# V's product in double groups with a twelve-slot ring of probabilities, and layer norms cut into stages

## The reference

```python
x = x + L0_xattn(layernorm(x), ctx)   # 8 heads of 8 channels, band |q-k| <= 64, gated with ctx
x = x + L0_ffn(layernorm(x))          # ternary 256x256 weight, tanh-scaled by the row norm
x = x + L1_xattn(layernorm(x), ctx)   # rotary, full 256x256 scores, keys and values of mixed origin
x = x + L1_ffn(layernorm(x))          # 256 -> 1024 -> 256, 4-bit weights with LoRA, relu

# attention, per sequence and head
scores = q @ k.T / sqrt(8);  p = softmax(scores);  o = p @ v
# layernorm
(x - mean) / sqrt(var + 1e-5)
```

## Time and profile before

| | us |
|---|---|
| three runs, median (lowest to highest) | 1336.01 (1335.77 to 1337.31) |
| the profiled execution | 1332.8 |
| its span | 1331.0 |
| TensorE's mean granted clock in it | 0.984 of full |

### The profile page before, as it was taken

One profiled execution on the slowest core, in us unless ns is written; L12 is line 12 of the kernel. 1 busy time (PEld: TensorE's weight loads), 2 busy tenths in 40 slices (PEclk: granted clock), 3 DMA queues, 4 the chain that ended last, 5 costly groups with the idle time before them and its releaser, 6 DMA issues.

```text
span 1331.0 us, 35488 instructions
## 1 busy us (share of the span) xinstructions
PE 1259.3 (95%) x11100; PEld 836.7 (63%) x11100; DVE 906.8 (68%) x1924; ACT 848.2 (64%) x1849; POOL 676.3 (51%) x1169
## 2 busy tenths in 40 slices
PE   6999999999999998768899999999999989999998
PEld 3667676767766765544565656666666546666665
DVE  6878878887888873659999988888888842111110
ACT  2566777767777775556888888888888853222111
POOL 4577788787878765055455445555555211000000
PEclk9999999999999998988999999999999999999999
DMA  8554555445544430033444444444454400000000
GB/s 208 121 135 106 117 119 117 103 117 116 116 113 112 102 85 6 13 80 89 93 105 94 96 95 103 112 103 101 103 113 99 85 2 16 16 16 16 16 16 32
DMA packets 90486, 113.34 MB, mean 85 GB/s; under 512 B 13971, under 2 KB 80275, under 8 KB 82739
## 3 DMA queue, kind: packets, MB, share of 16 engines
q1 hardware_dynamic: 89216, 111.25, 36.3%
q10 hardware_dynamic: 1206, 1.29, 0.3%
HBM read 18.66 MB, written 4.19 MB: 17 GB/s over the span
## 4 chain that ended last, share of the span: by engine, by line
PE 72%; DVE 9%; POOL 6%; issue 4%; ACT 3%; DMA 3%; SPq 1%; POOLq 0%; ACTq 0%; DVEq 0%
PE bank L477 13%; PE bank L437 12%; PE bank L453 11%; PE bank L699 8%; PE bank L690 8%; PE bank L435 5%; DVE row_max L1131 5%; POOL probs L1355 4%; PE bank L489 4%; PE bank L541 2%; PE bank L508 2%; DMA Ks<-Ks 1%; PE bank L648 1%; PE bank L518 1%; PE bank L529 1%
## 5 line engine op out<-in xcount | busy, mean ns | idle before, releaser
L1131 DVE TENSOR_REDUCE row_max<-bank 128x2 f32<-128x384 f32 (+1 forms) x1024 | 597.7, 616 | 110.5 <-PE bank L437 106.2
L735 ACT ACTIVATE probs<-bank 128x384 f32<-128x384 f32 (+1 forms) x1024 | 536.8, 542 | 162.2 <-PE bank L453 151.5
L437 PE MATMUL bank<-Ks,Qs 96*128 96x192 bf16 (+1 forms) x2048 | 372.1, 263 | 15.1 <-DVE row_max L1131 8.8
L453 PE MATMUL bank<-Qs,Ks 128*128 128x192 bf16 (+1 forms) x2048 | 365.6, 260 | 13.5 <-ACT probs L735 12.4
L1355 POOL TENSOR_SCALAR_AFFINE_SELECT probs<-probs 128x256 f32<-128x256 f32 (+1 forms) x512 | 259.3, 530 | 98.7 <-ACT probs L735 78.3
L437 PEld LDWEIGHTS bank<-Ks,Qs 96*128 96x128 bf16 x2048 | 186.7, 99 | 125.8 <-DVE row_max L1131 39.4
L477 PE MATMUL bank<-probs,V 128*32 128x192 f32 (+1 forms) x4096 | 248.3, 360 | 7.2 <-POOL probs L1355 5.9
L453 PEld LDWEIGHTS bank<-Qs,Ks 128*128 128x128 bf16 x2048 | 185.7, 97 | 45.4 <-ACT probs L735 31.7
L435 PE MATMUL bank<-band,ident 128*128 128x384 bf16 x512 | 168.6, 329 | 1.4 <-DMA Ks<-Ks 1.0
L477 PEld LDWEIGHTS bank<-probs,V 128*32 128x32 f32 x4096 | 107.3, 109 | 87.2 <-issue 43.8
L1292 DVE TENSOR_TENSOR X<-bank,X 128x256 f32 (+1 forms) x32 | 13.6, 424 | 185.6 <-PE bank L699 185.6
(11 more groups left out here) (114 smaller groups left out, 1614.3 us busy)
## 6 DMA issues: line engine op xcount, KB each, us to landing
Ks<-Ks SPq DMA_DIRECT2D x64, 576.0 KB
Qs<-Qs SPq DMA_DIRECT2D x128, 192.0 KB
Qs<-Qp SPq DMA_DIRECT2D x192, 64.0 KB
Ks<-Kp SPq DMA_DIRECT2D x192, 64.0 KB
X<-in_x SPq DMA_DIRECT2D x4, 1024.0 KB, 13.4
side<-in_ctx_crossed SPq DMA_DIRECT2D x32, 128.0 KB, 2.1
side<-in_ctx SPq DMA_DIRECT2D x32, 128.0 KB, 2.1
out<-X SPq DMA_DIRECT2D x8, 512.0 KB, 3.0
```

The source lines that it names most:

```text
L437: last = nc.tensor.matmul(dst[:, blk * win:(blk + 1) * win], Qs[0:SHIFT_ROW, pair[1], h, blk * P:(blk + 1) * P], Ks[0:SHIFT_ROW, pair[1], ...
L453: last = nc.tensor.matmul(dst[:, blk * win:(blk + 1) * win], Ks[:, pair[1], h, blk * P:(blk + 1) * P], Qs[:, pair[1], h, start(blk):start( ...
L735: nc.scalar.activation(probs[:, h % 8, 0:2 * win], exp_bank[h % 2][:, 0:2 * win], ACT.Exp, scale=SCALE).then_inc(s["exped"], 1)
L1131: nc.vector.tensor_reduce(row_max[:, pair[1], h // HEADS, 0, h % HEADS * 2:h % HEADS * 2 + 2], bank_of(pair, h)[:, 0:2 * win].rearrange("p ...
```

## The change

1. V's product runs two groups back to back. `values_half` issues groups 2 and 3 of the pair before at head 3 (layer 1: head 2), and groups 0 and 1 of this pair at head 11 (10). Groups 0 and 2 so come four heads later than before.
2. `probs` has twelve slots. An exp waits for the slots of three groups earlier. In the feed-forward of layer 0 its buffers lie in slots 8 to 11, so that DVE may begin there when the last pair's groups 0 and 1 are done; the scratch `junk` lies in `heads_sb`.
3. `q_rest` and `k_rest` have one copy instead of three; their writer waits for the reader of the pair before.
4. The norm's seven instructions are three stages (`norm_sums`, `norm_moments`, `norm_var`) with a semaphore of their own (`ln_step`), issued at successive heads; the root stands within the next pair (before exp 1 of pair 30 in both layers; before exp 2 of pairs 2 and 10 in layer 1), the inverse at head 8 or 5 of it.

```diff
+PROBS = 12
...
-        probs = sb("probs", [P, 8, 2 * T])
+        probs = sb("probs", [P, PROBS, 2 * T])
...
-        q_rest = sb("q_rest", [P, RING, T])
-        k_rest = sb("k_rest", [P, RING, T])
+        q_rest = sb("q_rest", [P, T])
+        k_rest = sb("k_rest", [P, T])
...
+        def slot_of(pair, h):
+
+            return (HPP * pair[1] + h) % PROBS
...
+            def values_half(pair, half):
+
+                for g in (2 * half, 2 * half + 1):
+                    values_group(pair, g)
...
-                    if h % 4 == VALUES_AT[l]:
-                        values_group(m1 if h < 4 else r, (h // 4 - 1) % 4)
+                    if h % HEADS == VALUES_AT[l]:
+                        values_half(m1 if h < HEADS else r, 1 - h // HEADS)
...
                 if h % 4 == 0:
-                    wait_some(e, s["pv_done"], num(pair) * 4 + h // 4 - 1)
+                    wait_some(e, s["pv_done"], num(pair) * 4 + h // 4 - PROBS // 4 + 1)
...
-        def scalar_edges(e, n):
-
-            if n == 1:
+        def scalar_within0(e, n, h):
+
+            if (n, h) == (TAIL_NORM + 2, 1):
+                e.wait_ge(ln_var, 3)
+                scalar_sqrt(0, TAIL_NORM)
+
+        def scalar_within1(e, n, h):
+
+            if (n, h) == (2, 2):
                 e.wait_ge(ln_var, 6)
                 scalar_sqrt(FIRST_CHUNK, SECOND_CHUNK)
-            if n == 9:
+            if (n, h) == (10, 2):
                 e.wait_ge(ln_var, 7)
                 scalar_sqrt(SECOND_CHUNK, PAIRS)
-            if n == TAIL_NORM + 1:
+            if (n, h) == (TAIL_NORM + 2, 1):
                 e.wait_ge(ln_var, 8)
                 scalar_sqrt(0, TAIL_NORM)
...
+        def late_norm(e, n, h, round_, pairs):
+
+            if (n, h) == (TAIL_NORM + 1, 12):
+                norm_sums(e, round_, 0, TAIL_NORM, ln_vec, pairs)
+            if (n, h) == (TAIL_NORM + 1, 13):
+                norm_moments(e, round_, 0, TAIL_NORM)
+            if (n, h) == (TAIL_NORM + 1, 14):
+                norm_var(e, round_, 0, TAIL_NORM)
+            if (n, h) == (TAIL_NORM + 2, 8):
+                vector_rstd(e, round_, 0, TAIL_NORM)
...
-                wait_some(e, s[f"{name}_parts"], num(pair) - RING + 1)
+                wait_some(e, s[f"{name}_parts"], num(pair))
...
-            e.wait_ge(L[0]["pv_done"], PAIRS * 4 - 1)
+            e.wait_ge(L[0]["pv_done"], PAIRS * 4 - 2)
```

More of the change, by code:

```diff
@@ L146, in build @@
         ff = sb("ff", [P, PAIRS, T])
-        ff0_xT = [probs[:, n // 2, n % 2 * T:(n % 2 + 1) * T] for n in range(FF0_RING)]
-        ff0_xn = [probs[:, 2 + n // 2, n % 2 * T:(n % 2 + 1) * T] for n in range(FF0_RING)]
-        junk = probs[:, 4, :].rearrange("p (a t) -> p a t", a=2)
+        ff0_xT = [probs[:, PROBS - 4 + n // 2, n % 2 * T:(n % 2 + 1) * T] for n in range(FF0_RING)]
+        ff0_xn = [probs[:, PROBS - 2 + n // 2, n % 2 * T:(n % 2 + 1) * T] for n in range(FF0_RING)]
+        junk = heads_sb[:, :].rearrange("p (a t) -> p a t", a=2)
         xT = (Ks[:, 0:2, :, :].rearrange("p a h t -> p (a h t)").bitcast(fp32)[:, 0:4 * T * 2]
@@ L478, in values_group @@
                                                 V[:, pair[1], column:column + 32],
-                                                probs[:, head % 8, blk * win:(blk + 1) * win],
+                                                probs[:, slot_of(pair, head), blk * win:(blk + 1) * win],
                                                 start=(g % 2 == 0 and blk == 0), stop=(g % 2 == 1 and blk == 1),
@@ L733, in exp_head @@
                 if h % 4 == 0:
-                    wait_some(e, s["pv_done"], num(pair) * 4 + h // 4 - 1)
-                nc.scalar.activation(probs[:, h % 8, 0:2 * win], exp_bank[h % 2][:, 0:2 * win], ACT.Exp,
+                    wait_some(e, s["pv_done"], num(pair) * 4 + h // 4 - PROBS // 4 + 1)
+                nc.scalar.activation(probs[:, slot_of(pair, h), 0:2 * win], exp_bank[h % 2][:, 0:2 * win], ACT.Exp,
                                      scale=SCALE).then_inc(s["exped"], 1)
@@ L751, in high_part @@
                     rest = q_rest if name == "q" else k_rest
-                    nc.scalar.activation(parts[:, u, 0, :], rest[:, u, :],
+                    nc.scalar.activation(parts[:, u, 0, :], rest[:, :],
                                          ACT.Copy).then_inc(s[f"{name}_high"], 1)
@@ L812, in iteration @@
                 for h in heads:
+                    if within and isinstance(r[0], int):
+                        within(e, num(r), h)
                     if h == 2 and l == 0:
@@ L908, in _ @@
             e.wait_ge(weights0_in, 2 * 16)
-            _, run, tail = scalar_attention(e, 0, scalar_prepare)
+            _, run, tail = scalar_attention(e, 0, scalar_prepare, scalar_within0)
             run(-AHEAD)
@@ L932, in tanh @@
                 nc.scalar.activation(tmp[:, 2, first:end], tmp[:, 1, first:end], ACT.Tanh).then_inc(f_tanh, 1)
-            iteration, run, next_tail = scalar_attention(e, 1, scalar_edges)
+            iteration, run, next_tail = scalar_attention(e, 1, None, scalar_within1)
             def between(n):
@@ L938, in between @@
                     tail[n]()
+                if n == FF0_LAG[1]:
+                    wait_job(e, L[0], 0, "A", "heads", TAIL, "filled")
                 if n == 8:
@@ L1026, in vector_rstd, with vector_norm @@
             e.wait_ge(ln_ready, round_)
-        def vector_norm(e, round_, first, end, vec, base):
-            vector_var(e, first, end, vec, base)
+        def vector_norm(e, round_, first, end, vec, pairs):
+            norm_sums(e, round_, first, end, vec, pairs)
+            norm_moments(e, round_, first, end)
+            norm_var(e, round_, first, end)
             vector_rstd(e, round_, first, end)
@@ L1087, in vector_within @@
                 ff0_update(e, FIRST_CHUNK + 5 * n + h // 3)
+            if n == 1 and h == 14:
+                norm_sums(e, 6, FIRST_CHUNK, SECOND_CHUNK, ff_vec, SECOND_CHUNK)
             if n == 1 and h == 15:
-                vector_var(e, FIRST_CHUNK, SECOND_CHUNK, ff_vec, SECOND_CHUNK + NORM_STEPS)
-            if n == 2 and h == 1:
+                norm_moments(e, 6, FIRST_CHUNK, SECOND_CHUNK)
+            if n == 2 and h == 0:
+                norm_var(e, 6, FIRST_CHUNK, SECOND_CHUNK)
+            if n == 2 and h == 5:
                 vector_rstd(e, 6, FIRST_CHUNK, SECOND_CHUNK)
@@ L1139, in rest_of @@
                 e.wait_ge(s[f"{name}_high"], num(pair) + 1)
-                wait_some(e, s[f"{name}_parts"], num(pair) - RING + 1)
-                nc.vector.scalar_tensor_tensor(out=rest[:, pair[1], :], in0=job_bank[bk][:, 0:T],
+                wait_some(e, s[f"{name}_parts"], num(pair))
+                nc.vector.scalar_tensor_tensor(out=rest[:, :], in0=job_bank[bk][:, 0:T],
                                                scalar=b[:, column:column + 1], in1=parts[:, pair[1], 0, :],
@@ L1235, in _ @@
             e.wait_ge(weights0_in, 2 * 16)
-            apply, _, run, tail = vector_attention(e, 0, vector_prepare)
+            apply, _, run, tail = vector_attention(e, 0, vector_prepare, vector_within0)
             apply((0, 0))
@@ L1251, in _ @@
             e.wait_ge(rope_in, 16)
-            apply, iteration, run, next_tail = vector_attention(e, 1, vector_edges, vector_within)
+            apply, iteration, run, next_tail = vector_attention(e, 1, None, vector_within)
             def between(n):
@@ L1321, in split @@
                     e.wait_ge(s[f"{name}_high"], num(pair) + 1)
[L1322 removed]
+                    nc.gpsimd.tensor_tensor(rest[:, :], rest[:, :], parts[:, u, 0, :],
                                             ALU.subtract).then_inc(s[mid], 1)
@@ L1340, in rot_sum @@
                 e.wait_ge(s["rot_mul"], num(pair) * 2 + n + 1)
-                wait_some(e, s[f"{name}_parts"], num(pair) - RING + 1)
-                nc.gpsimd.tensor_tensor(rest[:, pair[1], :], rot[:, 2 * n, :], rot[:, 2 * n + 1, :],
+                wait_some(e, s[f"{name}_parts"], num(pair))
+                nc.gpsimd.tensor_tensor(rest[:, :], rot[:, 2 * n, :], rot[:, 2 * n + 1, :],
                                         ALU.add).then_inc(s["rot_sum"], 1)
@@ L1349, in mask_group @@
                 wait_apart(e, (s["exped"], num(pair) * HPP + 4 * g + 4))
-                first = (g % 2) * 4
+                first = slot_of(pair, 4 * g)
                 half = P // 2
```

65 lines of the change are left out of this document (35 added, 30 removed).

## The result

| | us |
|---|---|
| the changed kernel, median of 4 runs | 1358.63 (1356.52 to 1360.06) |
| before, beside it, median of 4 runs | 1335.89 (1335.19 to 1337.31) |
| ratio, with its 95% interval | 1.0170 (1.0154 to 1.0186) |
| span of the profiled execution | 1358.3 (before 1331.0) |

Slower by 1.7%, some 23 us, and outside the range of 1300 to 1341: the forecast was 1319.4. The windows of the profile after that answer to the earlier trace rows have the same columns. Three are a pair of layer 0 each; then come one of pairs 2 to 9 and an ordinary pair of layer 1, and that ordinary pair's two stretches, from head 2's product to head 10's and from there to the next.

What follows compares the result with a forecast made beforehand. It took ACT and PE to pace layer 1's ordinary pairs in turn, DVE pairs 2 to 9. Terms 0-5.2-1.5-5-0.8-1.1-3 sum to -16.6 us, from the median 1336.01 to 1319.4; range 1300 to 1341, own range 1311 to 1329.

Steps and rivals of the forecast that it cites:

- layer 1, ordinary pairs: The 20 ordinary pairs of layer 1: gains and losses of the moved groups cancel, about 0, bounds -0.25 to +0.4.
- In the second stretch group 2 is gone from head 14: 1.09 us less, since PE sets the pace.: Layer 1, exp 11 to head 2's product: falls to 3.9 us, in which ACT needs 3.5.
- SP's transfers move with their pairs: DMA transfers issued by SP: listed among the rest of the change, with no cost given.
- ACT sets the pace of the first stretch: Layer 1, exp 2 to exp 10 of an ordinary pair: ACT is busy 7.44 of 7.60 us and sets the pace.
- The merged boundary: Entering and leaving 32-column tiles once less, twice a pair: 0.23 us each, 29 us of PE time over 64 pairs.
- rival D: The boundary stays: nothing of 29 us is saved, moves cost +6, late terms give -7: 1335 us, chance 0.12.
- Pieces of ACT's chain: Layer 1, ordinary pair: 5.1 from exp 3 through exp 8, +2.9, +3.5, +0.4 to the product, +2.8, adding to 14.7 us.
- Layer 1's pairs 2 to 9: Eight DVE-bound pairs of layer 1: DVE loses waits, the period falls from 15.5 to about 14.85, -5.2 us.
- Layer 0: Its 32 pairs: some of PE's saving is left despite DVE's lost catch-up, together -5 us, bounds +3 and -14.
- Late norms and clock: Roots at pairs 2, 10 and 30 of layer 1 -0.8 and -1.1, no clock fall -3; pair 30 of layer 0: 0.
- C: Long products starve ACT, exp 3 slips 0.86 in layer 1: +0.43 in 20 pairs, +11 in all, 1347 us, chance 0.19.
- B: PE is the bound everywhere: all 29 us come, and about 5 of norms and clock: 1302 us, chance 0.17.

Runs made afterwards that it cites:

- e2: Changed kernel with layer 1's transposition of the maxima of heads 0 to 7 ahead of head 10's product, ACT's copy and POOL's split earlier too: 1340.00 us.
- e8: Changed kernel with one merged boundary in layer 1: groups 2 and 3 together at head 2, group 0 at head 6, group 1 at head 10: 1337.94 us.
- e15: Changed kernel with, in layer 1, groups 0 and 1 together at head 10, group 2 at head 14, group 3 single at head 2: 1350.05 us.
- e3: Changed kernel with layer 1's ACT copy, the high part of k, moved from behind exp 8 to behind exp 10: 1357.32 us.
- e9: e2 with one of ACT's two copies of k's rotation left out in layer 1's loop, so part of the computation is missing: 1340.43 us.
- e11: e2 with layer 1's copy of the finished product to heads_sb moved from ACT to DVE, ahead of the maximum of head 3: 1343.87 us.
- e5: e2 with layer 1's rotation of k (ACT's two copies and DVE's product) moved from ahead of exp 5 to behind it: 1360.46 us.
- e12: e2 with DVE's product for layer 1's rotation of k put ahead of the maximum of head 5 instead of behind it: 1352.01 us.
- e14: e8 with e2's early maxima: 1326.73 us, ratio to before 0.9930.
- e1: Changed kernel with layer 1's four groups single again at heads 2, 6, 10 and 14, all else still changed: 1332.59 us.
- e10: Changed kernel with single groups in both layers, keeping slots, single rests and staged norms: 1337.13 us, ratio to before 1.0004.

## Why the prediction was wrong

**The step that failed** is "layer 1, ordinary pairs", which I took as 0 and which measured +1.2 us in each. Two of its parts did. In its own terms it put +0.4-0.12 = +0.28 us on the first stretch and +0.86-1.09 = -0.23 on the second; measured are +0.54 and +0.67. So 0.9 of the 1.2 us lie in the second stretch, and e2 won 0.57 of a pair back.

*"In the second stretch group 2 is gone from head 14: 1.09 us less, since PE sets the pace."* I checked ACT's need for the 3.9 us that were left from exp 11 to head 2's product, and not the transfer's. It took 4.8 (911.55 to 916.34). The DMA of the maxima, one row of SP's queue, was passed over with "SP's transfers move with their pairs". The trace of before held the room: issued at 911.33, needed at 913.92, 2.59 us. With the 2.32 us from issue to use that PE's waits show in the trace after and in e8, that was a slack of 0.27 us in a stretch from which I took 1.09. Shown by e2 and e8.

*"ACT sets the pace of the first stretch"*. This was right in part: with the product at head 6 gone PE does wait for exp 5 (e15). But ACT alone was not the bound, and not at exp 8, where I looked: e3 took work from behind exp 8, e9 and e11 from ahead of exp 5, and all won nothing. That the term came out only 0.26 us off is partly luck. What I missed is what the product at head 6 covered: two waits, of head 7 for exp 5 and of the turn back for DVE's use of bank B, that end within 0.3 us of each other. The trace of before held both:

```profile
905.33 0.60 ACT L735 ACTIVATE probs<-bank 128x512 f32<-128x512 f32 x1
...
905.58 0.47 DVE L1159 SCALAR_TENSOR_TENSOR rot<-bank,att_b,rope 128x256 f32<-128x256 f32 x1
...
906.17 0.38 PE L453 MATMUL bank<-Qs,Ks 128*128 128x256 bf16 x2
906.39 0.38 PE L552 MATMUL bank<-ident,normed 128*128 128x128 f32 x2
```

Exp 5 ended 0.24 us ahead of head 7's scores and DVE's rotation 0.34 ahead of the turn back, and I took 1.09 us of work from in front of both. That this product covers 0.9 us is shown by e15 beside e8; that the two waits end nearly together by e5 and e9, where each time the other one took over. What each wait is worth by itself stays open, since e12, which shortened DVE's part, brought a new delay with it.

**The terms by themselves.**
- The merged boundary, 0.23 us: right. A double product takes 1.87 us from start to next start (916.34 to 918.21; forecast 1.86), and rival D falls. The saved PE time, 29 us by the forecast's rows, was lost again in waits.
- Pieces of ACT's chain that I had right: head 2's product to exp 3 took 2.79 (forecast 2.8), exp 3 to the end of exp 8 5.2 (5.1), on to exp 11 3.1 (2.9), ACT idle 1.81 behind head 10's product (1.7). A chain whose pieces are right is still wrong where another one ends later.
- Layer 1's pairs 2 to 9: 15.7, forecast 14.85. Their stretches take 8.50 and 7.23 us, before 8.39 and 7.11, and e2 has 15.2. DVE did not lose waits: busy 14.54 of 15.70, it idles 1.16 where it idled 0.96. e14 shows the term with the covers in place: 15.03 to 15.10.
- Layer 0: forecast -5, measured -0.3 over 27 pairs, nothing outside the noise of e1 and e10; plain pairs 14.87 instead of 14.6, with unpacking 15.26 as forecast. There too PE now waits for the transfer: 3.3 us in ten waits from 135 to 435 us, none before. No run moves the maxima in layer 0, so what this costs there is not shown.

```profile
PE bank L459 <- DMA Qs<-max_rows: 3.3, 10, 0.7
```

- Late norms and clock, -4.9: in part. At pair 30 of layer 1 PE stood under 1 us (0.70 and 0.33) and the clock stayed at 1.00, as forecast. In none of the 13 traces with a double product at head 2 of layer 1 does a low clock follow here; with a single one it does, behind a stand of 1.56 us in e1, e10 and e15 and of 2.83 before. At pairs 2 and 10 the root costs 1.9 and 2.2 us where it cost 2.8, forecast -0.4 each. In layer 0, where I had put 0, PE now stands 0.55 and 1.73 us (before 2.21), the granted clock is 0.83 from 490 to 500 us, where it was 1.00, and from head 11 to head 11 pair 30 takes 17.5 for 16.1. The change alone does not decide this: e1, whose code for layer 0 is the same, stands 0.54 and 1.74 us there, keeps the clock at 1.00 and takes 16.1.

```profile
1092.45 0.39 PE L459 MATMUL bank<-Qs,Ks 128*128 128x256 bf16 x2 [0.70 <-ACT probs L746]
...
495.57 0.50 PE L459 MATMUL bank<-Qs,Ks 128*128 128x192 bf16 x2 [1.73 <-ACT probs L746]
```

The window of these 10 us, the clock third from the end:

```profile
490.00:500.00 10.00, 7.57 (x71) 4.40 (x70) 4.96 (x14) 7.23 (x13) 4.02 (x8) 0.83 0.07 17
```

**The rivals.** C had the sign (pairs above 15, as it said) and one part of the mechanism, PE waiting for exps behind a long product, but priced it at 0.43 a pair and put it at exp 3, which came when I had forecast it. B was 57 us off. None had the transfer.

## What to carry to other kernels

Long work on the bound engine is also a cover: before moving it, list every round trip that starts and ends around its place (maxima to DMA to use; turn, other engine, turn back) and take its length from the trace, start of the first to start of the last; where it exceeds the work that stays, the difference is lost at once. Neither a neighbour's busy share of 98% nor the absence of waits tells how much can be taken away: PE waited for nobody, and the three things that it came to wait for had been ready 0.24 to 0.34 us ahead of their use. And start a long latency early before counting on room elsewhere: moving one transposition by two heads, with its split and copy, was worth 18 us, and together with a smaller merge it turned the loss into 0.7% of gain.
